# A rotation of VectorE ahead of three field passes, the passes one slot later, in a two-layer transformer kernel

## The reference, cut to what matters

```python
# field: one step of a reaction-diffusion equation on the sequence, seen as a 256x256 image
lap_x = yp_x[:, :, :-2] - 2.0 * y + yp_x[:, :, 2:]
lap_y = yp_y[:, :-2, :] - 2.0 * y + yp_y[:, 2:, :]
du_dt = zX * lap_x + zY * lap_y + zR * y * (1.0 - y)
# attention on it: RMS norm, projections, rotation by position
x = seq * rsqrt(mean(seq * seq, -1) + eps) * g_norm
q, k, v = split(x @ W_qkv)                 # 16 heads of 64
q = q * cos + rotate_half(q) * sin         # the same for k
# in segments of 128 rows, with 16 learned keys and values in front
attn = softmax(where(mask, q @ k.T / 8, -1e30))
out = (attn @ v) @ W_out
x_next = y + out
```

## Time and profile before

| | |
|---|---|
| three runs | 2426.37, 2429.45, 2429.3 us; median 2429.3 |
| the profiled execution | 2426.79 us, its span 2424.7 us |
| mean granted TensorE clock | 0.975 |
| TensorE busy in the span | 2248.6 us (93%) |
| VectorE busy | 1852.2 us (76%) |
| ScalarE busy | 1292.3 us (53%) |
| GpSimd busy | 1019.9 us (42%) |

### The profile page before, as it was taken

One profiled execution on the slowest core, in us unless ns is written; L12 is line 12 of the kernel. 1 busy time (PEld: TensorE's weight loads), 2 busy tenths in 40 slices (PEclk: granted clock), 3 DMA queues, 4 the chain that ended last, 5 costly groups with the idle time before them and its releaser, 6 DMA issues.

```text
span 2424.7 us, 53715 instructions
## 1 busy us (share of the span) xinstructions
PE 2248.6 (93%) x18240; PEld 2041.3 (84%) x18240; DVE 1852.2 (76%) x5119; ACT 1292.3 (53%) x3839; POOL 1019.9 (42%) x1078
## 2 busy tenths in 40 slices
PE   3799999999976899999999999899999999999999
PEld 2688878888865778888888887899999999999999
DVE  5878888888878666666666765578878888888876
ACT  1667666666662455655555554433336555555522
POOL 5535454454525455455555553033332222222073
PEclk8999999999997899999999999999999999999999
DMA  4523333333330322222222222222126777777443
GB/s 138 182 85 107 103 95 116 91 113 95 99 110 3 99 57 58 72 60 58 70 64 57 66 57 75 64 36 43 39 94 213 233 235 237 233 232 239 142 120 124
DMA packets 203301, 267.36 MB, mean 110 GB/s; under 512 B 61670, under 2 KB 171510, under 8 KB 192278
## 3 DMA queue, kind: packets, MB, share of 16 engines
q1 hardware_dynamic: 194166, 245.27, 33.4%
q0 software_dynamic: 8864, 18.66, 2.9%
HBM read 175.84 MB, written 43.94 MB: 91 GB/s over the span
## 4 chain that ended last, share of the span: by engine, by line
PE 58%; DVE 19%; POOL 8%; issue 7%; ACT 6%; DMA 1%; SPq 0%; POOLq 0%; DVEq 0%; ACTq 0%
PE bank L55 48%; PE bank L136 6%; POOL P L1796 2%; DVE xe L928 2%; PE bank L1322 2%; DVE Ph L821 2%; DVE tb L1654 1%; DVE qm L917 1%; DVE xe L933 1%; DVE sgs L955 1%; ACT P L1495 1%; PE bank L1362 1%; ACT Ph L657 1%; DVE rot0s L881 1%; DVE hb L965 1%
## 5 line engine op out<-in xcount | busy, mean ns | idle before, releaser
L1495 ACT ACTIVATE P<-P,mx 128x144 f32<-128x144 f32 x512 | 206.2, 405 | 229.2 <-DVE mx L1616 228.2
L2642 POOL DMA_INDIRECT xE<-d_y,ixs x78 | 112.1, 1437 | 336.2 <-PE bank L136 300.7
L55 PE MATMUL bank<-xD_hi,w1e_lo 128*128 128x256 f32 x880 | 251.1, 285 | 0.0
L55 PE MATMUL bank<-w2e_hi,hrD_hi 128*128 128x256 f32 x880 | 249.0, 283 | 0.0
L55 PE MATMUL bank<-w2e_lo,hrD_hi 128*128 128x256 f32 x880 | 248.9, 283 | 0.0
L55 PE MATMUL bank<-w2e_hi,hrD_lo 128*128 128x256 f32 x880 | 248.9, 283 | 0.0
L55 PE MATMUL bank<-xD_lo,w1e_hi 128*128 128x256 f32 x880 | 245.9, 279 | 0.0
L55 PE MATMUL bank<-xD_hi,w1e_hi 128*128 128x256 f32 x880 | 245.6, 279 | 0.0
L1127 POOL TENSOR_TENSOR xe<-xe 128x704 f32<-128x704 f32 (+3 forms) x64 | 88.0, 1375 | 353.9 <-DVE xe L936 353.7
L1796 POOL TENSOR_TENSOR P<-P,rs 128x512 f32<-128x512 f32 x128 | 133.1, 1040 | 246.0 <-DVE rs L1625 243.5
L2251 ACT ACTIVATE hD<-bank,b1E 128x256 f32<-128x256 f32 x312 | 127.0, 473 | 197.2 <-PE bank L55 182.8
(11 more groups left out here) (324 smaller groups left out, 7959.7 us busy)
## 6 DMA issues: line engine op xcount, KB each, us to landing
w1raw<-in_ew SPq DMA_DIRECT2D x39, 1024.0 KB, 5.9
w2raw<-in_ew SPq DMA_DIRECT2D x39, 1024.0 KB, 4.9
stack<-d_rot SPq DMA_DIRECT2D x256, 96.0 KB, 2.7
K<-Kn SPq DMA_DIRECT2D x256, 72.0 KB, 2.0
d_rot<-QKh SPq DMA_DIRECT2D x64, 256.0 KB, 3.1
Q<-Qn SPq DMA_DIRECT2D x256, 64.0 KB, 2.0
d_ys<-oE SPq DMA_DIRECT2D x39, 256.0 KB, 2.6
d_rot<-QKl SPq DMA_DIRECT2D x32, 256.0 KB, 3.1
```

The costliest lines, as they stand in the source:

```text
L55: inst = e.matmul(out, l, r, start=k == 0, stop=k == len(pairs) - 1)
L1495: inst = e.activation(P1[t % 2][:, n, :], P1[t % 2][:, n, :], ACT.Exp, bias=mx1[t % 2][:, 2 * g + sg:2 * g + sg + 1], scale=-1.0, accum_ou ...
L2642: e.indirect_dma_start(out=xE[q % 2][c], out_offset=None, in_=d_y, in_offset=bass.IndirectOffsetOnAxis(ap=ixs[r % 4][:, c:c + 1].bitcast(U ...
```

## The change

In slot 1 the three field passes behind `copy_turned` give their place to rotation 2. In slot 2 rotation 3 takes the place of rotation 2 ahead of `maxima`, and the field passes take the place of rotation 3 behind `maxima`. Nothing is added or dropped, and the lists of TensorE, ScalarE, GpSimd and SyncE are the same as before.

```diff
                     if s == 2:
-                        rotate(b + 1, 2)
+                        rotate(b + 1, 3)
                     if s == 4:
                         normalize(entering(b))
...
                     if s == 0:
                         rotate(b + 1, 0)
                     if s == 2:
-                        rotate(b + 1, 3)
+                        field(entering(b))
+                        field_sum(entering(b))
                     if s == 5:
                         rotate(b + 1, 6)
                     copy_turned(t)
+                    if s == 1:
+                        rotate(b + 1, 2)
                     if s == 4:
                         rotate(b + 1, 4)
                     if s == 7:
                         differences(entering(b + 1))
-                    if s == 1:
-                        field(entering(b))
-                        field_sum(entering(b))
```

## The result

| | before | after |
|---|---|---|
| median | 2429.45 us (5 runs, 2426.37 to 2430.24) | 2415.63 us (5 runs, 2408.54 to 2419.02) |
| ratio | | 0.9939, 95% interval 0.9928 to 0.9949 |
| profiled execution, its span | 2426.79, 2424.7 us | 2417.32, 2415.3 us |
| mean granted TensorE clock | 0.975 | 0.968 |
| one block (norm of block 1 to norm of block 13, over 12) | 44.92 us | 43.57 us |

The change makes the kernel faster by 0.6%, some 14 us. One execution of experiment 9 was slow, 5412.8 us with TensorE's matmuls of 0.54 us where the other runs have 0.28, and is left out of every figure here.

What follows compares the result with a forecast made beforehand. TensorE was taken as the bound, near dense, idling before the back projection for a bank VectorE's rotation 2 frees late. Terms -15.0 + 2.6 + 0.6 = -11.8 gave 2415.0 us, plus 2.5 to the median 2417.5; range 2411 to 2425.

Steps and rivals of the forecast that it cites:

- What goes: Blocks 1 to 13: TensorE's back projection no longer waits 1.34 us for its bank; at most 1.38 us a block.
- The company of GpSimd: Slot 2 behind the maxima: passes alternate with GpSimd's combine pieces, a piece begun during a pass stretching by 0.33 us.
- 1.15 a block, 15.0 in all: Blocks 1 to 13: maxima of slot 3, and the norm behind them, come 1.15 us earlier in each block.
- the undisturbed case: Rival: passes not disturbed by GpSimd; 17.6 us go, the head costs 1.7, in all -15.9, 2413.4 us; chance 0.23.
- The head, +2.6: Block -1: passes behind rotation 3 end later, so TensorE's sum of squares and what follows come 2.6 us later.
- Block 0, +0.6: Block 0 has no back projection to gain; its later passes start ScalarE's square 0.6 us later.
- The sum: Whole kernel: -15.0 + 2.6 + 0.6 = -11.8 us, taking the profiled 2426.8 us to 2415.0.
- The step from one profiled execution to the median, +2.5: Median of the runs shown lay 2.5 us above the profiled execution, so 2415.0 became 2417.5 us.
- The dearer exchange: Rival: a GpSimd piece stretches by a whole pass, 0.75 us; +1.3 in all, 2430.6 us, no change; chance 0.13.
- GpSimd's pieces first: Rival: GpSimd runs its four combine pieces before the passes get in; +20.6 us, 2449.9 us, slower; chance 0.06.

Runs made afterwards that it cites:

- experiment 9: Kernel before with rotation 2 alone moved up behind the copy of slot 1, run once more on one chip with the changed kernel: median 2409.6 us, ratio 0.9925.
- experiment 2: Kernel before with rotation 2 alone moved behind the copy of slot 1, passes staying in slot 1 behind it: 2410.36 us, ratio 0.9932.
- experiment 4: Changed kernel with GpSimd's combines 2 and 3 moved behind the normal of slot 3, from block 1 on: 2414.3 us, ratio 0.9949.
- experiment 6: Kernel before with rotation 2 alone moved behind the copy of slot 1, plus one more field pass in blocks 1 to 13: 2417.8 us, ratio 0.9944.
- experiment 3: Kernel before with the three field passes alone moved, from slot 1 to behind rotation 3 in slot 2: 2419.22 us, ratio 0.9968.
- 1: Changed kernel with the order of before in blocks -1 and 0, the new order from block 1 on: 2412.66 us, ratio 0.9941.
- experiment 7: Kernel before with one more field pass ahead of the last, in blocks 1 to 13: 2448.79 us, ratio 1.0082 to before.
- 5: Changed kernel with one more field pass ahead of the last, in blocks 1 to 13: 2432.06 us, ratio 1.0002 to before.
- 8: Changed kernel, unaltered, run once more on one chip with the kernel that moves rotation 2 alone: 2415.08 us, ratio 0.9941.

## Why the prediction was right, and where it was not

The forecast of 2417.5 us lies 1.9 above the median, the whole range of the runs but the two fastest lies in 2411 to 2425, and its mechanism is the one that the traces show. By its steps:

**What goes.** Right. `back` finds its bank free in all 13 blocks.

**The company of GpSimd.** Right, step by step. Three of four pieces stretch by 0.33 (0.73 to 1.06), as the one pair in the earlier trace rows had it for a larger shape; pass 3 ends 6.9 us after the copy of slot 1, where 6.97 was foreseen. The Trainium skill, "SBUF — State Buffer", "Who interferes with whom", states the exclusion; the runs agree, with passes of 1.10 us beside the pieces and 0.75 where GpSimd is idle (experiment 2).

**1.15 a block, 15.0 in all.** The size was off: the trace gives 1.36, some 17.6. The copy came 0.08 earlier than foreseen, I let the maxima follow it by 0.51 where they follow by 0.42, and the norm gained 0.04 more on the maxima (5.83 to 5.79). That the disturbance is nearly free, though, was not in the prediction: it priced the undisturbed case 0.2 a block lower, and experiment 4 shows 0.03, because TensorE's scores set the maxima 0.08 us below.

**The head, +2.6.** The sum of squares came 2.62 us later, counted from L1127 (9.01 to 11.63): this step is exact, with rotation 3 0.97 earlier (1.0 foreseen) and the passes alternating. The size of the term was still off: 3.48. The missing 0.86 lie behind the squares, where I had let everything "follow". From there to VectorE's sum into `X` (L995) it takes 7.17 us before and 8.03 after. TensorE has no idle time between the squares and the end of the down projection in either; what differs is how long it works at 1.2 GHz:

| kernel | start of the squares, after L1127 | clock 1.00 reached, after that start | squares to L995 |
|---|---|---|---|
| experiment 2 | 9.03 us | 1.5 us | 6.18 us |
| experiment 6 | 9.03 | 3.6 | 7.13 |
| before | 9.01 | 3.7 | 7.17 |
| experiment 3 | 11.64 | 4.5 | 7.53 |
| after | 11.63 | 5.6 | 8.03 |
| experiment 4 | 11.65 | 5.7 | 8.06 |

(the clock is worked out from the mean clock of the window in which it changes). Experiments 2 and 6 have the same order there and start the squares at the same place, yet differ by 0.95 us. Their windows from 794 to 796 us, with the squares begun at 793.54 and 793.17:

```profile
794.00:796.00 2.00, 2.00 (x11) 1.70 (x11) 0.58 (x3) 1.65 (x3) 1.14 (x2) 0.74 0.00 0
794.00:796.00 2.00, 2.00 (x8) 1.73 (x8) 0.21 (x2) 1.45 (x3) 0.77 (x2) 0.50 0.00 0
```

Experiment 3 and after form a second such pair (0.50 us). So the length follows the clock and not the start of the squares. What sets the moment of its rise no run shows; before and three runs with its start (1, 6, 7) have 3.6 to 3.7, and all four with the order of after (after, 4, 5, 8) 5.6 to 5.7.

**Block 0, +0.6.** From the copy of slot 1 to the norm it took 16.30 us before (822.65 to 838.95) and 16.90 after (830.77 to 847.67): 0.60, and ScalarE's square starts later by the same 0.60, as foreseen.

**The sum.** -17.6 + 3.5 + 0.6 = -13.5, against -11.8 foreseen; two errors, 2.6 of gain and 0.9 of cost, partly cancelled; that the forecast lies so near the median is in part luck. The trace from L1127 to the norm of block 13 shortens by the same 13.5 (640.91 to 627.41). The profiled executions differ by less, 9.5 us, because in that of after the first layer ran 4.6 us longer up to L1127 (782.61 against 787.25) with the same instructions. Its granted clock was lower, 0.75 and 0.88 in the first two stretches of 60 us against 0.81 and 0.93 in that of before; that this is the cause is not shown. The step from one profiled execution to the median, +2.5, thus rested on nothing firmer than this scatter.

**The rivals.** The undisturbed case gave nearly the right time, and with 1.35 a block a better price than the forecast's 1.15, for the wrong reason: the passes are disturbed, and it costs almost nothing. The dearer exchange and GpSimd's pieces first did not occur: VectorE got in behind each piece.

## What to carry to other kernels

When an in-order engine holds up a bank, move the short instruction that frees it, and ask whether the long work must move at all: here half of the change was better than the whole, because the head then kept its order (4.0 us from L1127 to the norm of block 0); that the passes kept their quiet place gave only some 0.04 a block. A wait that appears or goes on the busiest engine counts only if the chain passes through it; 1.09 us on TensorE cost nothing (experiment 2), and 1.00 us less of VectorE gained 0.03 a block (experiment 4). To learn how much room a place has, put one more instruction of the same kind there: the same pass cost 0.56, 1.14 or 1.74 us by its place (the last with a fall of the clock).

## What the runs showed of the hardware that was not expected

An idle time of 2.1 us on TensorE was followed in eight of 12 places by some 3.3 us at 1.2 GHz (matmuls of 0.41 us from about 1062.9 to 1066.2), and in four by none; idle times of 1.27 (experiment 6) and 1.34 us (before) left the clock at 2.4 GHz. So such a wait costs 1.5 us more than its length, or not; what decides between the two is not shown. And up to L1127 the same instructions ended up to 4.6 us apart in the profiled executions (782.61 to 787.25), with mean clocks of 0.74 to 0.88 in the first 60 us. These clocks alone do not explain it: at 0.88 (experiment 6) and 0.74 (experiment 7) L1127 starts at 784.14 and 784.02.
